# A chunked delta-rule recurrence: the state read through a compact inverse, one load record per step

## The reference, cut to what matters

```
KiT = swapaxes(Ki)
T   = tril(Bi @ KiT, k=-1)             # Bi = beta * k
inv = linalg.inv(eye + T)
Ui  = inv @ (Vi - Bi @ W_t)            # Vi = beta * v
W_new     = W_t + KiT @ Ui
W_avg_new = coef1 * W_avg + coef2 * W_t + KiT @ (Ui * w_i)
O_i = Qi @ W_avg * a + Qi @ W_t * c + T_mat * (Qi @ KiT) @ Ui
```

## Time and profile before

| | us |
|---|---|
| median of 3 executions | 1509.95 |
| lowest and highest | 1496.23, 1513.25 |
| the profiled execution's own time | 1498.91 |
| its span in the profile | 1497.1 |

### The profile page before, as it was taken

One profiled execution on the slowest core, in us unless ns is written; L12 is line 12 of the kernel. 1 busy time (PEld: TensorE's weight loads), 2 busy tenths in 40 slices (PEclk: granted clock), 3 DMA queues, 4 the chain that ended last, 5 costly groups with the idle time before them and its releaser, 6 DMA issues. The chain is left out here.

```text
span 1497.1 us, 35306 instructions
## 1 busy us (share of the span) xinstructions
PE 1164.3 (78%) x14558; PEld 796.8 (53%) x14558; DVE 749.3 (50%) x1707; ACT 452.9 (30%) x889; POOL 321.9 (22%) x309
## 2 busy tenths in 40 slices
PE   4843765665655067778887878999999999999997
PEld 2632434434444056666676764665566666666664
DVE  4689999899999436754444453112111121211111
ACT  3540534424435022222332323331122222222221
POOL 3686101000000011110011104661022222222222
PEclk9875777778778557687888878999999999999999
DMA  7642555464556676567665619952132222223222
GB/s 272 189 145 63 147 153 116 132 162 103 143 111 158 160 158 152 130 143 165 157 148 141 160 56 342 346 167 78 28 47 47 46 47 44 46 47 47 47 46 29
DMA packets 232444, 184.00 MB, mean 123 GB/s; under 512 B 148165, under 2 KB 196197, under 8 KB 227937
## 3 DMA queue, kind: packets, MB, share of 16 engines
q1 hardware_dynamic: 198000, 149.20, 38.0%
q0 software_dynamic: 16368, 19.96, 7.6%
q10 hardware_dynamic: 17920, 12.59, 3.1%
HBM read 101.69 MB, written 86.26 MB: 126 GB/s over the span
## 5 line engine op out<-in xcount | busy, mean ns | idle before, releaser
L1420 DVE TENSOR_TENSOR hid_all<-p_s,silu 128x512 f32<-128x512 f32 x103 | 71.3, 692 | 378.5 <-PE p_s L1271 249.7
L1470 POOL DMA_INDIRECT out_h<-y_sb,x_in x71 | 110.8, 1560 | 360.7 <-DVE y_sb L1432 342.8
L1328 ACT ACTIVATE silu<-p_m 128x512 f32<-128x512 f32 x103 | 61.5, 597 | 328.2 <-PE p_m L1264 223.4
L175 DVE TENSOR_TENSOR xt<-xt,prod 128x62 f32<-128x62 f32 (+15 forms) x248 | 151.8, 612 | 4.3
L1286 PE MATMUL p_y<-wo,hid_all 128*128 x568 | 134.4, 380 | 0.8 <-ACT hid_all L1345 0.8
L1264 PE MATMUL p_m<-wi,xT_c 128*128 x284 | 133.6, 593 | 0.5 <-ACT xT_c L1341 0.5
L1271 PE MATMUL p_s<-ws,xT_c 128*128 x284 | 133.6, 593 | 0.0
L172 DVE TENSOR_TENSOR prod<-nx,xt 128x62 f32<-128x62 f32 (+15 forms) x248 | 129.6, 523 | 2.6
L577 DVE SCALAR_TENSOR_TENSOR cv<-raw,conv_sb,cv 128x512 f32<-128x512 f32 x144 | 107.0, 747 | 18.0 <-ACT raw L493 17.2
L1286 PEld LDWEIGHTS p_y<-wo,hid_all 128*128 128x128 f32 x568 | 102.5, 190 | 12.3 <-issue 1.4
L452 PE MATMUL p_g<-kqM,kT 32*32 32x128 f32 x2048 | 50.7, 369 | 71.2 <-DVE sT L647 53.8
(11 more groups left out here) (139 smaller groups left out, 1938.0 us busy)
## 6 DMA issues: line engine op xcount, KB each, us to landing
slots_in_dram<-h SPq DMA_DIRECT2D x9, 1040.0 KB, 10.0
x_in<-slots_in_dram SPq DMA_DIRECT2D x71, 130.0 KB, 2.1
k_tokens_dram<-kk SPq DMA_DIRECT2D x32, 256.0 KB
chunk_gram_dram<-ng SPq DMA_DIRECT2D x32, 256.0 KB
beta_kv_dram<-bv SPq DMA_DIRECT2D x32, 256.0 KB
nx<-chunk_gram_dram SPq DMA_DIRECT2D x8, 1024.0 KB, 4.9
xt<-in_const SPq DMA_DIRECT2D x8, 1024.0 KB, 8.0
scores_dram<-sT SPq DMA_DIRECT2D x32, 256.0 KB
```

Of the source, the lines that this page charges most:

```text
L175: ins = dve.tensor_tensor(kept, kept, pr, ALU.add)
L1420: dve.tensor_tensor(dst, p_s[n % 2][:], silu[n % 2][:], ALU.mult).then_inc(S["hid_ready"], 1)
L1470: pool.indirect_dma_start(token_rows, bass.IndirectOffsetOnAxis(x_in[s % X_IN][:, D:D + 1].bitcast(U32), 0), y_sb[s % 2][:], None, compute ...
```

## The change

Stage B no longer multiplies the inverse by beta-k and beta-v ahead of time. It reads the state with beta-k first, adds beta-v, and applies the inverse to the sum: `read_k`, `rho_out`, `apply`. The inverse stays compact (32 by 32 tiles) and is used in 64 small tile matmuls as `inside` uses the scores. `kk`, scores, inverse and beta-v of a step lie in one record of 1792 floats per token row and are loaded by one DMA into one of three buffers. Beta-k goes to stage B by channels: stage A transposes it (`turn_beta_k`), ScalarE evicts it negated, and SP stores it as it stores q; `load_kq` loads it with q (12 DMAs instead of 8). `turn_o` moves behind `grow`, `turn_xn` ahead of `project`; VectorE's `norm` goes to the next step's start and `residual` to the step's end.

```diff
+AT_KK, AT_SCORES, AT_INVERSE, AT_BV, RECORD = 0, 2 * D, 2 * D + H * C, 2 * D + 2 * H * C, 3 * D + 2 * H * C
...
-    x_dram = nc.dram_tensor("chunk_inverse_dram", [NC_BATCH, B, C, H * C], F32, kind="Internal").ap()
+    step_dram = nc.dram_tensor("step_records_dram", [NC_BATCH, B, C, RECORD], F32, kind="Internal").ap()
+    kT_dram = nc.dram_tensor("beta_k_channels_dram", [B // GROUP, TILES, 4 * DH, GROUP, HQ, P], F32, kind="Internal").ap()
...
+                        by_chunk(AT_SCORES, b, sT[:].rearrange("p t g x -> p t (g x)"), H * C)
+                        sp.wait_ge(s_nk, b * 2 + 2)
+                        by_slot(kT_dram, b, nkT)
...
                         if n >= 2:
                             pe.wait_ge(s_raw, b * 6 + n - 1)
                         elif b:
-                            pe.wait_ge(s_kt, (b - 1) * 2 + n + 1)
-                            pe.wait_ge(s_ktri, (b - 1) * TILES + 2 * (n + 1))
+                            pe.wait_ge(s_nk, (b - 1) * 2 + n + 1)
...
+                    def turn_beta_k(b):
+                        for u in range(2):
+                            pe.wait_ge(s_kt, b * 2 + u + 1)
+                            pe.wait_ge(s_ktri, b * TILES + 2 * (u + 1))
+                            pe.wait_ge(s_bk, b * 2 + u + 1)
+                            for s in range(4):
+                                t, k = 2 * u + s // 2, s % 2
+                                ins = pe.transpose(p_p[u][:, s * P:(s + 1) * P], bk[:, t, k * P:(k + 1) * P], ident)
+                            ins.then_inc(s_bkt, 1)
...
                         gram(b, 1)
+                        turn_beta_k(b)
...
+                        for u in range(2):
+                            act.wait_ge(s_bkt, b * 2 + u + 1)
+                            act.activation(nkT[:, :, 2 * u * P:(2 * u + 2) * P].rearrange("p k (t l) -> p t k l", t=2),
+                                           p_p[u][:].rearrange("p (t k l) -> p t k l", t=2, k=KH), ACT.Copy, scale=-1.0
+                                           ).then_inc(s_nk, 1)
...
+                    def load_record(s):
+                        if s >= RING:
+                            sp.wait_ge(S["o_summed"], s - RING + 1)
+                        sp.dma_start(record[s % RING][:], step_dram[chunk(s), b:b + GROUP].rearrange("b i x -> (b i) x")
+                                     ).then_inc(s_rec[s % RING], 16)
-                        if s == 14:
+                        if s == 12:
                             store_inverse(sp, B - 1)
-                        load_yz(s)
-                        load_kk(s)
-                        load_scores(s)
+                        load_record(s)
...
...
+                    def read_k(s):
...
+                        pe.wait_ge(S["state_ready"], 2 * states(s - 1))
+                        for n in range(HQ):
+                            for b in range(GROUP):
+                                ins = pe.matmul(p_rf[lane(b), n * 4 * DH:(n + 1) * 4 * DH], nk[n4 % 2][:, b, n, tok],
+                                                state[s % 2][:, b, n, :], start=(n == 0), stop=True, skip_group_check=True)
...
+                    def apply(s):
+                        pe.wait_ge(s_rec[s % RING], 16 * (s // RING + 1))
+                        pe.wait_ge(S["rho_ready"], reads(s))
+                        pe.wait_ge(S["u_ready"], s)
+                        for hd in range(H):
+                            for b in range(GROUP):
+                                ins = pe.matmul(p_u[lane(b), hd * DH:(hd + 1) * DH], xT[s % RING][lane(b), hd, :],
+                                                src[lane(b), hd * DH:(hd + 1) * DH], start=(hd == 0), stop=True, skip_group_check=True)
...
                     for s in range(NT + 4):
+                        if s < NT:
+                            read_k(s)
                         if s >= 4:
                             route(s - 4)
                         if s < NT:
-                            read_y(s)
+                            apply(s)
                             read_q(s)
+                            grow(s)
                         if 1 <= s <= NT:
                             turn_o(s - 1)
                         if s < NT:
-                            grow(s)
-                            if s + 1 < NT:
-                                yz(s + 1)
                             inside(s)
+                        if 2 <= s < NT + 2:
+                            turn_xn(s - 2)
                         if 1 <= s <= NT:
                             project(s - 1)
-                        if s + 1 < NT:
-                            take_z(s + 1)
-                        if 2 <= s < NT + 2:
-                            turn_xn(s - 2)
...
+                        dve.tensor_tensor(rho[s % 2][:], p_rf, bv[s % RING], ALU.add).then_inc(S["rho_ready"], 1)
...
                     for s in range(NT + 4):
+                        if s < NT:
+                            rho_out(s)
+                        solve(SHARE * s)
+                        if 2 <= s < NT + 2:
+                            norm(s - 2)
                         if s >= 4:
                             gate(s - 4)
-                        solve(SHARE * s)
+                        solve(SHARE * s + 2)
                         if s < NT:
                             state_out(s)
+                            solve(SHARE * s + 4)
                             head_sum(s)
-                        solve(SHARE * s + 2)
+                            solve(SHARE * s + 6)
+                            head_norm(s)
                         if 1 <= s <= NT:
                             residual(s - 1)
-                        solve(SHARE * s + 4)
-                        if s < NT:
-                            head_norm(s)
-                        solve(SHARE * s + 6)
-                        if 1 <= s <= NT:
-                            norm(s - 1)
```

More of the change, by code:

```diff
@@ L87, in consts @@
     add("own_head", (p[:, None] // C) == (np.arange(4 * DH)[None, :] // DH))
-    add("pick_z", (p[:, None] // C * DH + p[:, None] % C - DH == np.arange(4 * DH)[None, :]) & (p[:, None] % C >= DH))
     add("rms_eps", np.full((P, 1), 1e-6))
     add("ln_eps", np.full((P, 1), 1e-5))
-    add("minus_y", np.where(p[:, None] % C < DH, -1.0, 0.0))
     row = np.arange(32)
@@ L619, in _ @@
                         for u in range(2):
-                            beta_times(b, 1, u)
+                            beta_v(b, u)
                             solve(b - 1, 4 + u, 5 + u)
@@ L667, in build @@
             rms_sb = sb(ctx, "rms_sb", [P, 1])
-            bv = pair_of("bv_b", [P, H, 2 * DH])
-            kk = pair_of("kk_b", [P, H, 2 * DH])
-            sT = pair_of("sT_b", [P, H, C])
-            xbd = pair_of("xbd", [P, H, P])
+            RING = 3
+            record = [sb(ctx, f"record{i}", [P, RECORD]) for i in range(RING)]
+            kk = [r[:, AT_KK:AT_SCORES].rearrange("p (h d) -> p h d", h=H) for r in record]
+            sT = [r[:, AT_SCORES:AT_INVERSE].rearrange("p (h i) -> p h i", h=H) for r in record]
+            xT = [r[:, AT_INVERSE:AT_BV].rearrange("p (h i) -> p h i", h=H) for r in record]
+            bv = [r[:, AT_BV:RECORD] for r in record]
+            nk = pair_of("nk", [P, GROUP, HQ, P])
             qq = pair_of("qq", [P, GROUP, HQ, P])
-            yz_ch = pair_of("yz_ch", [P, HQ, P])
-            y_ch = pair_of("y_ch", [P, HQ, P])
+            rho = pair_of("rho", [P, D])
             u = pair_of("u", [P, D])
@@ L716, in states, with reads @@
                 return s // NC_BATCH * (NC_BATCH - 1) + min(chunk(s) + 1, NC_BATCH - 1)
-            def k_loads(s):
-                return sum(1 for e in range(s % 2, s + 1, 2) if chunk(e) < NC_BATCH - 1)
+            def reads(s):
+                return s // NC_BATCH * (NC_BATCH - 1) + chunk(s)
             def lane(n):
@@ L728, in _, with load_kq @@
                         sp.dma_start(dst, src).then_inc(s_weights, 16)
-                    def load_q(n):
+                    def load_kq(n):
                         if n >= 2:
                             sp.wait_ge(S["o_summed"], TILES * (n - 1))
+                        i = n % 2
+                        for f in range(4):
+                            sp.dma_start(nk[i][C * f:C * f + DH], kT_dram[n // TILES, n % TILES, f * DH:(f + 1) * DH]).then_inc(s_nk[i], 16)
                         for f in range(4):
@@ L783, in _ @@
                     for i in range(2):
-                        pool.memset(xbd[i][:], 0.0).then_inc(s_zeroed, 1)
-                    def scale_q(n, b):
+                        pool.memset(nk[i][:], 0.0).then_inc(s_zeroed, 1)
+                    for n in range(NT // TILES):
                         t = n % TILES
-                        pool.wait_ge(s_qq[n % 2], 16 * 8 * (n // 2 + 1))
-                        pool.tensor_tensor(qq[n % 2][:, b], qq[n % 2][:, b],
```

(25 more changed lines are left out.)

167 lines of the change are left out of this document (72 added, 95 removed).

## The result

The changed kernel takes 1587.7 us (median of 4, 1586.1 to 1590.0); the kernel before, run beside it, 1506.7 us (4 runs, 1496.2 to 1513.3). The ratio is 1.055, 95% interval 1.048 to 1.061: it is slower, by 81 us. Ratios compare executions in the chip's usual state, and one of b4_nodma's four (1673 us, at a granted clock of 0.69) is left out for that. The profiled spans are 1588.2 and 1497.1 us.

A forecast was written before the change was run, and what follows sets the result against it. VectorE was taken to bound stage A, TensorE's order stage B. Stage A +4, stage B's start -9 and body 0 gave -5; leaning up by 8 made +3 on 1510, so 1513 us, range 1484 to 1546.

The forecast's parts named there:

- term (a): Stage B step, TensorE's work: `yz`, `take_z`, `read_y` go, `read_k` and `apply` come: -0.66 us per step.
- (b): Stage B step: 64 more instruction pairs make TensorE wait for instruction blocks: +0.94 us per step, bounds 0 and +1.83.
- (e): Stage B step, DMA load: small packets go, so instruction fetches come sooner: -0.3 us per step, bounds 0 and -0.7.
- (c): Stage B step: `apply` newly waits for VectorE's `rho_out`: +0.6 us per step, bounds 0 and 1.2.
- its overlap: Stage B step: an instruction block can land during the wait of (c), so (b) and (c) don't add fully: -0.3 us.
- (d): Stage B step: waits of `turn_o` behind `gate` and `read_q` behind `head_norm` go, 0.39 us per step saved.
- leaned upwards by 8 us: Whole forecast: 8 us added because less of stage B may run at 2.4 GHz.
- Rival 1: Stage B: instruction supply sets the pace, every `apply` waits the full 1.83 us; +30 us, 1540 us; chance 0.33.
- The body's lower bound, -36: Stage B over 31 steps: lowest change allowed by the bounds of (b), (c) and (e); highest +43 us.
- Stage A: Stage A and its stores: projections between the first two sequences 2 us later, SP's last stores 2 us: +4 us.
- Rival 2: Stage B: DMA load caused the late instruction blocks, so the change is faster: -31 us, 1479 us; chance 0.18.
- less clock: Outcome further off on the slow side than the forecast and rivals, with a lower clock; no time given; chance 0.04.

The follow-up runs named there:

- b4_nodma: Kernel before without the recurrence's loads after the first two steps, old operands used again (values wrong): ratio 0.9775 to the kernel before.
- b1: Kernel before with 32 more matmul calls of 16 columns (64 pairs) per step ahead of the block-diagonal product, result overwritten: ratio 1.0345.
- a3: Changed kernel loading only the first three records and first two sets of beta-k and q, then reusing them (values wrong): ratio 1.0204 to the kernel before.
- a7: Changed kernel with both operands of `apply` read as bfloat16, 64 pairs fewer per step: ratio 1.0083 to the kernel before.
- a8: Changed kernel with `apply` in bfloat16 and without the loads after the third record, both together: ratio 0.9758 to the kernel before.
- b5: b3 plus two wide matmuls of 256 columns per step ahead of its read pass, result unused: ratio 1.0004 to the kernel before.
- b6: Kernel before plus two wide matmuls of 256 columns per step ahead of its read of the state: ratio 1.002.
- a6: Changed kernel plus four wide matmuls per step, two ahead of `inside` and two ahead of `apply`, result unused: ratio 1.0558 to the kernel before.
- b3: Kernel before with `take_z` and `read_y` merged into one pass over a mixed state that VectorE writes, 32 pairs fewer per step: ratio 1.0083.
- a2: Changed kernel with each step's record loaded by four DMAs with rows of at most 2 KB instead of one with 7 KB: ratio 1.0434.
- a1: Changed kernel with its twelve loads of beta-k and q spread over three steps, four in each: ratio 1.0636 to the kernel before.
- a0_again: The changed kernel run once more, nothing altered: ratio 1.0493 to the kernel before.

## Why the prediction was wrong, point by point

The forecast was 1513 us, with a range to 1546; it came to 1587.7. The body was forecast at 0 and took +85.3 us (some 10 of them the fast execution before). Its three parts:

| body | forecast | measured |
|---|---|---|
| TensorE busy: term (a), clock as it was | -20 | +53 |
| waits for instructions: (b) and (e), 0.94 - 0.3 per step | +20 | +51 |
| waits for other engines: (c), its overlap, (d), +0.6 - 0.3 - 0.39 | -3 | -19 |

1. **Term (a), work at the old clock: the assumption that failed most.** I summed (a) with durations at 0.73 and 0.82 and leaned upwards by 8 us. The clock fell to 0.58, and busy time came out 73 us above the sum. Seven groups stand in both bodies with the same matmuls (`inside`, `project`, `grow`, `read_q`, `route` and the two turns); by the views by form they took 212 us before and 273 after, so 61 of the 73 us are old work made slower. The prediction did say that the clock might fall, and gave it a tenth of its size. Of its two reasons, waits that lower the clock are refuted by b1 (more waits, 0.77) and by a3, a7 and a8 (fewer waits, 0.58). The other, that the wide `yz` goes, is half right: full-width calls bring the clock back in b5, b6 and in part in a6 (0.72), but b3 lost as much of it with `yz` in place. Which of the old matmuls had held it up in this kernel stays open. Not all of the 73 us is lost time: while TensorE runs slowly it uses up its instructions more slowly, and in b5 the waits rose by 13 us when the clock came back, little more than the 10 that repeat badly.

2. **Term (b), about right.** Without loads the waits are 30.9 us before (b4) and 52.0 after (a3): +21, or 0.68 us per step; b1 gives 0.83 with the old loads, a7 0.49 with the new ones. The forecast was 0.94, a little above them all. Rival 1's 1.83 was too much for pairs alone.

3. **Term (e), the sign was wrong: no relief came.** I took the end of the small packets for relief, -0.3 us per step. The loads' part of the waits went from 18 to 49 us instead, +1.0 per step, 40 us off the forecast; by the ratios their worth went from 34 to 44 or 52 us, a rise hardly beyond the noise, where a fall of 9 was forecast. The stops of 8.00 and 7.87 us in the rows above lie under full DMA engines. Which property of the new loads does it stays open: records in four pieces with rows of at most 2 KB gave back 7 to 15 us (a2), spreading the burst nothing (a1).

   The Trainium skill ("Runtime: NRT & Kernel Launch", "Instruction fetch mechanics") has the fetch mostly hidden. No run here agrees: 100.7 us of the changed kernel's body are waits for blocks, and 52.0 even with its loads gone (a3).

4. **Terms (c) and (d): the new wait costs nothing, the old ones went.** `apply` never waited for `rho` in the profile. In a typical step VectorE was done with it while `route` still ran, and `apply` followed on `route` at once:

```profile
797.75 1.02 PE L905 MATMUL p_turn<-router_sb,xnT 128*128 128x8 f32 x4
797.89 0.42 DVE L1014 TENSOR_TENSOR rho<-p_r,record 128x256 f32<-128x256 f32 x1
798.70 1.16 PE L835 MATMUL p_u<-rho,record 32*32 32x16 f32 x72
```

   The prediction had said "nothing at half clock", and half clock is nearly what came. All other waits fell from 19.4 to 0.5 us. The body's lower bound, -36, keeps (c) at 0.6; with (c) at its own bound of 0 the sum gives -54.

5. **Stage A and the start: +4 and -9 both failed to come.** The body's beginning hides this, since the two moved against each other. SP's first DMA of stage B left at 511.14, where it was 515.89, and the window from the first record's issue on was this:

```profile
511.14 0.34 SPq L761 DMA_DIRECT2D wout_in<-in_wout  x1
512.48:541.00 28.52, 8.94 (x446) 8.28 (x448) 8.96 (x20) 2.35 (x4) 6.43 (x6) 0.50 0.88 204
```

   So stage A ended 4.8 us earlier and not 4 later; but over the profiles on the faster chips that moment lies anywhere from 503 to 516 us in kernels of either sort, so a +4 is neither shown nor excluded. From there to U of step 1 it took 30.1 us, and 27.7 before: +2.4, where -9 was forecast. The first record came at 520, and the loads behind it ran at 204 GB/s and not at the 265 that I took; and `apply` of step 0 stopped for 7.87 us before its last 5 matmuls, which is step (e) again.

6. **Rival 1** (instruction supply, 1540) named the right engine and the right wait, and fell short by 48 us: it kept the clock and left (e) at nothing. Its sign that decides, a block that takes longer than 3.6 us to come, is met by single waits under load (up to 8.00); the time from request to landing stands in no view. **Rival 2** has the right cause for a large part of the waits and the wrong sign. Its own gain would need the loads gone: that is worth 2.3% in the kernel before (b4) and takes the changed one from 1.055 to 1.020 (a3). The chance for "less clock", 0.04, was the one that came, together with rival 1.

What stays open: the split between clock and waits in the changed kernel is not sharper than about 10 us (a0_again), and no run gave its body the old clock at no cost.

## What to carry to other kernels

Price a change to a dense stage of small tiles three times over: in work, in instructions, and in what it does to TensorE's clock. 64 matmul and load pairs more or fewer in a step were worth 50 to 70 us over 31 steps, more than half of it their own busy time and the rest waiting; and where small tiles took the place of `yz` and `take_z`, the clock fell by a quarter, which made the old work 61 us longer. Tidying loads into few large ones didn't relieve the instruction supply here: look at the longest "issue" wait and at the DMA share beside it, not at the number of packets.

## What the runs showed of the hardware

- Two full-width matmul calls in each step brought the granted clock after the tenth step from 0.62 to 0.82 and made TensorE's busy time fall by 28 us, although they added 48 us of work (b3_merge, b5_merge_wide). 32 narrow calls in each step (128*32, 16 columns), 35 us of work, left the clock of the body at 0.77 (b1_pairs).
- The changed kernel's body, in which TensorE is busy for 77% of the time and seven of ten matmuls are 32 by 32 tiles, was granted 0.58, near the lower level of 1.2 GHz (0.50); with the loads gone and 86% busy (a3_nodma) it was the same.
- The changed kernel stops for instructions mostly at distances of 127 matmuls or a multiple (380 in the rows above), and at the same matmuls with and without its loads; one such stop took 0.95 us without them and 8.00 with the DMA engines' share near 1. In the quiet part of a3_nodma the longest was 2.5 us.
- Not every matmul slows with the clock alike: from 0.78 to 0.58 the mean of a 32*128 matmul with 64 columns rose from 310 to 417 ns, that of a 32 by 32 tile with 16 columns from 191 to 208.
